# Who makes the low half of the transposed activations: GpSimd or VectorE

## The reference, cut to what matters

```python
mod = (_silu(L0_c) @ L0_wmod).reshape(L0_c.shape[0], 6, 1, -1)
h = _layernorm(x, axis=-1) * (1 + ca) + sa
# _L0_attn_ref(h, ...):
Q = _feature_map(x @ Wq.T + bq); K = _feature_map(x @ Wk.T + bk)   # elu + 1
V = x @ Wv.T + bv
KV = jnp.einsum('bshd,bshe->bhde', K, V)
K_sum = K.sum(axis=1)
Z = 1.0 / (jnp.einsum('bshd,bhd->bsh', Q, K_sum) + 1e-06)
out = jnp.einsum('bshd,bhde,bsh->bshe', Q, KV, Z) @ Wo.T + bo
```

## Time and profile before

| | us |
|---|---|
| median of 3 runs (354.36 to 356.01) | 354.59 |
| the profiled execution | 354.88 |
| its span, first to last instruction | 353.2 |
| TensorE busy | 337.2 (95%) |
| VectorE busy | 283.2 (80%) |
| GpSimd busy | 252.2 (71%) |
| ScalarE busy | 229.7 (65%) |

### The profile page before, as it was taken

One profiled execution on the slowest core, in us unless ns is written; L12 is line 12 of the kernel. 1 busy time (PEld: TensorE's weight loads), 2 busy tenths in 40 slices (PEclk: granted clock), 3 DMA queues, 4 the chain that ended last, 5 costly groups with the idle time before them and its releaser, 6 DMA issues.

```text
span 353.2 us, 7901 instructions
## 1 busy us (share of the span) xinstructions
PE 337.2 (95%) x2487; PEld 316.0 (89%) x2487; DVE 283.2 (80%) x795; ACT 229.7 (65%) x507; POOL 252.2 (71%) x334
## 2 busy tenths in 40 slices
PE   8888999999999997799999999999999999999895
PEld 8666877877888987799999999999999999999895
DVE  4589777657788789998989999898889887886753
ACT  4566778887877755755748558566585585765441
POOL 4348787868977577988879898898899966755210
PEclk9989999999999999999999999999999999999999
DMA  7956510000000033223232232322432333224311
GB/s 262 333 155 182 181 57 0 0 1 2 2 0 1 3 120 122 74 79 119 70 116 90 63 116 90 97 92 62 132 100 65 108 89 105 91 71 141 106 47 59
DMA packets 23998, 31.79 MB, mean 90 GB/s; under 512 B 2310, under 2 KB 14490, under 8 KB 23964
## 3 DMA queue, kind: packets, MB, share of 16 engines
q1 hardware_dynamic: 23524, 31.34, 28.6%
q10 hardware_dynamic: 440, 0.04, 0.1%
HBM read 27.04 MB, written 4.34 MB: 89 GB/s over the span
## 4 chain that ended last, share of the span: by engine, by line
PE 77%; DVE 9%; ACT 6%; POOL 4%; issue 4%; DVEq 0%; POOLq 0%; ACTq 0%
PE bank L867 20%; PE bank L868 20%; PE bank L869 19%; PE bank L875 5%; PE bank L907 4%; PE bank L1048 2%; PE bank L952 2%; PE bank L899 1%; PE bank L1090 1%; ACT tr_f L659 1%; DVE hid_g L1425 1%; POOL rstd L442 1%; ACT e_sb L683 1%; DVE stats L1192 1%; POOL tr_lo L461 1%
## 5 line engine op out<-in xcount | busy, mean ns | idle before, releaser
L805 ACT ACTIVATE bank<-bank,cols_sb 128x256 f32<-128x256 f32 x128 | 51.5, 440 | 49.3 <-PE bank L869 49.1
L867 PE MATMUL bank<-tr_hi,w_hi 128*128 128x256 f32 x256 | 72.7, 284 | 0.0
L869 PE MATMUL bank<-tr_hi,w_lo 128*128 128x256 f32 x256 | 71.6, 280 | 0.0
L868 PE MATMUL bank<-tr_lo,w_hi 128*128 128x256 f32 x256 | 71.6, 280 | 0.0
L867 PE MATMUL bank<-w_hi,hid_pair 128*128 128x256 f32 x252 | 70.8, 281 | 0.0
L868 PE MATMUL bank<-w_lo,hid_pair 128*128 128x256 f32 x252 | 70.6, 280 | 0.0
L869 PE MATMUL bank<-w_hi,hid_pair 128*128 128x256 f32 x252 | 70.6, 280 | 0.0
L552 POOL TENSOR_TENSOR hid_pair<-hid_g,hid_pair 128x512 fp32r<-128x512 f32 x42 | 54.8, 1306 | 4.4 <-ACT hid_pair L812 2.9
L867 PEld LDWEIGHTS bank<-tr_hi,w_hi 128*128 128x128 f32 x256 | 48.5, 189 | 0.3 <-DVE hid_g L1425 0.2
L868 PEld LDWEIGHTS bank<-tr_lo,w_hi 128*128 128x128 f32 x256 | 48.3, 189 | 0.0
L869 PEld LDWEIGHTS bank<-tr_hi,w_lo 128*128 128x128 f32 x256 | 48.2, 188 | 0.0
(11 more groups left out here) (171 smaller groups left out, 910.0 us busy)
## 6 DMA issues: line engine op xcount, KB each, us to landing
g_bc<-g_dram SPq DMA_DIRECT2D x64, 256.0 KB, 3.6
x_sb<-in_x SPq DMA_DIRECT2D x16, 256.0 KB, 3.7
out<-x_sb SPq DMA_DIRECT2D x15, 256.0 KB, 2.3
early<-in_wmod SPq DMA_DIRECT2D x3, 512.0 KB, 6.1
q_sb<-in_w SPq DMA_DIRECT2D x2, 512.0 KB, 6.4
q_sb<-in_w SPq DMA_DIRECT2D x1, 1024.0 KB, 9.4
mod_row<-mod_dram SPq DMA_DIRECT2D x1, 1024.0 KB, 6.3
q_sb<-in_wqkvT SPq DMA_DIRECT2D x2, 256.0 KB, 4.7
```

The source lines that it names most:

```text
L805: last = ac.activation(half, half, ACT.Gelu, bias=b1_sb[:, e:e + 1])
L867: te.matmul(out_ap, l_hi, r_hi, start=start, stop=False, skip_group_check=shared)
L868: te.matmul(out_ap, l_hi, r_lo, start=False, stop=False, skip_group_check=shared)
L869: return te.matmul(out_ap, l_lo, r_hi, start=False, stop=stop, skip_group_check=shared)
```

## The change

`split_lo` goes from GpSimd's program. VectorE's `split_a` makes the low half right behind the high half, and is now called for every unit: for units 9 to 15, whose high half is ScalarE's, it waits for ScalarE (`a_hi_end`) and makes the low half alone. The semaphores that the others wait for stay the same.

```diff
@@ GpSimd
-            def split_lo(u):
-                h = u.h
-                if cast_late(u):
-                    wait(pool, a_hi_end, u.count(1, 1) - (UPB + 1))
-                else:
-                    wait(pool, a_hi, u.count(1, 1))
-                wait(pool, a_qk, u.count(2, -2))
-                gp.tensor_tensor(tr_lo[:, h, :, :], tr_f[:, h, :, :], tr_hi[:, h, :, :].bitcast(F32), ALU.subtract)\
-                  .then_inc(a_lo, 1)
...
-                if u.plus(1):
-                    split_lo(u.plus(1))
@@ VectorE, split_a
                 wait(dve, a_hf, u.count(1, 1))
                 wait(dve, a_qk, u.count(2, -2))
-                ve.tensor_copy(tr_hi[:, h, :, :], tr_f[:, h, :, :]).then_inc(a_hi, 1)
+                if cast_late(u):
+                    wait(dve, a_hi_end, u.count(1, 1) - (UPB + 1))
+                else:
+                    ve.tensor_copy(tr_hi[:, h, :, :], tr_f[:, h, :, :]).then_inc(a_hi, 1)
+                    wait(dve, a_hi, u.count(1, 1))
+                TT(tr_lo[:, h, :, :], tr_f[:, h, :, :], tr_hi[:, h, :, :].bitcast(F32), ALU.subtract).then_inc(a_lo, 1)
@@ VectorE, step_a
-                if u.plus(1) and not cast_late(u.plus(1)):
+                if u.plus(1):
                     split_a(u.plus(1))
```

## The result

The changed kernel takes 357.75 us (median of 6 runs, 357.25 to 358.14) against 354.61 for the kernel before: 1.0082 times as long, 95% interval 1.0064 to 1.0100. It is slower by 3.1 us; 356.4 was forecast, in a range of 352.0 to 359.0.

What follows compares the result with a forecast made beforehand. TensorE was taken to bound the kernel, through its projection-stage gaps. Terms 0 + 0.8 + 1.3 + 0.3 + 0.5 - 1.4 + 0.3 gave +1.8 us: 356.7 for the profiled execution, 356.4 as median, range 352.0 to 359.0.

Steps and rivals of the forecast that it cites:

- What bounds: Projection stage: the change is worth what it does to TensorE's few gaps, 4.8 us of waits for GpSimd's low half.
- The disturbance: VectorE on SBUF: a large GpSimd instruction holds off a subtraction; the 512-element low half ends 0.56 us behind it.
- The small power: GpSimd's 4-element power: by the trace holds no VectorE work; by the page's rule low halves 3 and 11 wait 0.5 us.
- Rival B: The holds don't decide, fewer collisions in sum: 3.3 us gained, 351.3 us, faster; chance 0.14.
- GpSimd is there first by 0.1 to 0.2: Units 5 and 7: the K sum precedes the low half and holds it, +0.65 us each; -0.4 each if VectorE is first.
- The hold of the weight split: Units 6 and 8: delayed sums and biases hold the weight split, which passes 0.15 us on each, +0.3 together.
- rival A: VectorE wins the race in units 5 and 7: 2 x 1.05 us less, 354.3 us; chance 0.22.
- The gain of 0.8 at `place_kv`: Steps 9 and 10: products start 1.3 us earlier, `place_kv` is free, the 0.80 us idle ahead of L1006 goes.
- The gain at `keep_shifts`: Steps 9 and 10: its 1.24 us beside a GpSimd instruction now long done; `kv_of` had waited 0.5 us for it.
- units 10, 13, 14 and 15: within slack: These late units lose 0; VectorE's stand behind ScalarE's high half holds back only what already waited for the exponential.
- rival C: A hold in every unit, low halves of units 11 to 15 too: 2.5 us on top, 358.9 us; chance 0.14.
- rival D: The low half was hidden, another wait of equal length replaces its end at once: 354.6 us; chance 0.08.

Runs made afterwards that it cites:

- experiments 2 and 9: 2: changed kernel, only GpSimd's first K sum waits for unit 2's low half, 356.87 us; 9: changed kernel, VectorE making only low halves 1 to 8, 356.41 us.
- Experiment 8: The changed kernel with one 8-element memset more on GpSimd ahead of the K sum of step 4 alone: 357.77 us.
- experiment 1: The changed kernel with GpSimd's K sum, and all behind it, waiting in each step until VectorE's low half is made: 351.9 us.
- experiment 10: The changed kernel with GpSimd making the low halves of units 1 to 8 as before, VectorE those of units 9 to 15: 355.07 us.

## Why the prediction was right, and where its sizes were off

**What bounds.** TensorE's gaps in the projection stage alone set the price. Right: the rest of the span kept its length within 0.1 us.

**The disturbance.** Right in kind and size. A 512-element low half behind a large GpSimd instruction ends 0.55 behind it (0.56 foreseen). L1276 of the constants (L1284 before) was held at 23.48, as foreseen for step 1. The rows of the kernel after, GpSimd and VectorE in step 1, against the earlier trace rows:

```profile
23.41 1.29 POOL L458 TENSOR_TENSOR hid_g<-hid_g,k_sb 128x512 f32<-128x512 f32 x1
...
23.48 1.36 DVE L1276 TENSOR_SCALAR q_sb<-q_sb 64x256 f32<-64x256 f32 x1
```

It took 0.28 us before and 1.36 now. The small power did not hold a low half: that of unit 3 took its 0.69 us with the power running from 31.75 to 32.93 (kernel after, VectorE, then GpSimd):

```profile
32.40 0.69 DVE L1227 TENSOR_TENSOR tr_lo<-tr_f,tr_hi 128x512 fp32r<-128x512 f32 x1
...
31.75 1.18 POOL L442 TENSOR_TENSOR rstd<-var_eps,minus_half 128x4 f32<-128x4 f32 x1
```

Unit 11's came just behind its power, so that case didn't arise. By the Trainium skill, SBUF — State Buffer, section "Who interferes with whom", whoever issues first has the shared pair for the whole instruction, so that unit 3's low half would have waited to the power's end; the trace decides against that rule for such tiles.

**The sum of the holds.** Rival B argued that 19 us of GpSimd work less make fewer collisions in sum. For VectorE that came true: its busy time without the low halves fell by 1.1 us. The kernel became slower all the same, since the holds moved to places that TensorE waits for.

**Unit by unit.** Units 1 to 6, 9 to 11, 14 and 15 are within 0.25 us of their forecast each. The four that are not:
- *Unit 7* (the step "GpSimd is there first by 0.1 to 0.2"). The margins were 0.02 us in step 4 and -0.05 in step 6, so the steps went apart: +0.68 and -0.40. The step failed since the small last instruction of the deviations (L444), 0.20 us before, was itself held by the cast to 0.47 and 0.40, which the prediction did not count. It ended 0.05 and 0.06 behind the cast. That ties GpSimd's arrival to the end of the cast, where the low half arrives too. The margins are no accident of one execution: experiments 2 and 9 show the same 0.02 and -0.05. Experiment 8 shows that the order of arrival decides, and nothing else that differs between the steps. That unit 5 went as foreseen is luck by the same measure, a margin of 0.02.
- *Unit 8* (foreseen +0.15, measured +0.87). What unit 7 escaped came here: GpSimd's K sum took 1.77, its two sums and biases ran until 61.96, and the cast of unit 8 was held. Timeline of the kernel after, VectorE and GpSimd:

```profile
61.05 1.19 DVE L1225 CAST tr_hi<-tr_f 128x512 fp32r<-128x512 f32 x1 [0.24 <-ACT tr_f L646]
...
60.49 1.47 POOL L464 TENSOR_TENSOR x_sb<-x_sb,mod_row 128x512 f32<-128x512 f32 x1
```

  The hold of the weight split, which the prediction named for this unit, passed nothing on: the cast behind it still waited 0.24 us for ScalarE. Units 7 and 8 together were foreseen at +0.8 and lost 0.47. So rival A (VectorE wins a race) gave less than its price: 1.05 from one race came back by two thirds in the next unit.
- *Unit 12* (foreseen -0.5, measured +0.24). The gain of 0.8 at `place_kv` did not come. The products did start earlier, but the K sum of unit 10, next in GpSimd's queue, moved up as well, to the place where they had been. The rows of the kernel after, against the earlier trace rows:

```profile
83.81 1.28 POOL L458 TENSOR_TENSOR hid_g<-hid_g,k_sb 128x512 f32<-128x512 f32 x1
...
84.18 1.19 DVE L1345 TENSOR_TENSOR early<-early,head_mask 128x256 f32<-128x256 f32 x1
...
85.48 0.51 PEld L993 LDWEIGHTS bank<-wo_sb,early 128*128 128x128 f32 x3 [0.64 <-issue]
```

  The idle time ahead of `make_m` fell from 0.80 to 0.64 only. With GpSimd behind the low half (experiment 1) the gain is there: `place_kv` takes 0.42 us, and unit 12 wins 0.73.

```profile
80.20 0.42 DVE L1347 TENSOR_TENSOR early<-early,head_mask 128x256 f32<-128x256 f32 x1
...
80.83 0.73 PEld L995 LDWEIGHTS bank<-wo_sb,early 128*128 128x128 f32 x4
```

  The low half of unit 12 was held by `make_qz` (1.54 us), as foreseen. The gain at `keep_shifts` did come: L1302 took 0.23 us, and unit 11 won 0.69.
- *Unit 13* (foreseen 0, measured +0.86), and with it the step "units 10, 13, 14 and 15: within slack". Its low half asked at 94.13, and the K sum had come at 94.02:

```profile
94.13 1.70 DVE L1227 TENSOR_TENSOR tr_lo<-tr_f,tr_hi 128x512 fp32r<-128x512 f32 x1 [0.49 <-ACT tr_hi L654]
...
94.02 1.27 POOL L458 TENSOR_TENSOR hid_g<-hid_g,k_sb 128x512 f32<-128x512 f32 x1
...
96.62 0.19 PEld L854 LDWEIGHTS bank<-hid_pair,tr_hi 128*128 128x128 f32 x1 [0.99 <-DVE tr_lo L1227]
```

  Here rival C was right for one unit: a large instruction that has started just before the low half asks. Units 14 and 15 were within slack. Unit 10 was not quite: it lost 0.18, and as much in experiment 1, without holds. In the changed kernel the exponential was ready at 75.34, but the low half ended at 75.65 and the map started at 75.57. So the low half did keep the map back by some 0.2 us, which the prediction had ruled out.

**The sum.** +1.8 was foreseen, and the unit starts give +3.1; unit 12 (0.74), unit 13 (0.86) and the pair 7 and 8 (-0.33) make 1.27 of the 1.31 missing. The mechanism, its main places and the sign were right, the size was a little over half. The median came out 1.35 us above the forecast for the same reasons. Rival B (holds don't decide) is refuted by experiment 1, rival D by the table. B's price of 3.3 us for a change without holds was nearly right as a size: experiment 1 has 2.7.

**What stays open.** Experiment 1 has GpSimd wait in every step. Whether a wait in fewer steps, those alone in which a hold reaches TensorE, would do better than 351.9 was not tried. The 0.10 us at unit 1 is explained in part: TensorE's weight load starts 0.12 us behind the end of the feature map, which now ends last, where it had started 0.05 behind the low half; why is not shown.

## What to carry to other kernels

When work leaves an engine, ask what that engine will do in its place: its queue moves up, and here the instructions that moved up cost the kernel more than the move gained (5.8 us against 2.7). The sum of the holds doesn't show it, as that hardly changed; their places do. Between GpSimd and VectorE on SBUF, keep large GpSimd instructions out of the moment in which VectorE has work that TensorE waits for; one semaphore wait that orders them was worth 5.85 us, though it adds idle time. Margins of some 0.1 us in such an order could not be forecast from durations here, so price both outcomes, and look for what a dodged hold hits next.

## What the runs showed of the hardware

- Which of the two engines is held follows the order of arrival down to 0.02 to 0.05 us: 44.12 against 44.14 gave GpSimd 1.27 and VectorE 1.80; 56.14 against 56.09 and, in experiment 8, 44.02 against 43.99 gave VectorE 0.69 and GpSimd 1.77 and 1.80. In the traces of all the runs together a low half on VectorE and a GpSimd instruction on 128 x 512 start within 0.15 us of each other 27 times; each time the one recorded second is the one that is held.
- GpSimd gives way between two instructions in a row: with the low half of unit 5 waiting, the K sum ended at 45.39, the low half at 45.94, and the next GpSimd instruction, recorded from 45.35, took 1.72 instead of 1.29.
- A 4-element GpSimd instruction can be held by VectorE's cast (0.47 instead of 0.20 us) and by its low half (0.75, experiment 10), though it holds neither: the cast took 0.43 and the low half 0.69.
- A VectorE instruction that was held ended as long behind GpSimd's each time: 0.54 to 0.55 us for the 512-element low half (units 5, 9, 12 and 13), 0.28 to 0.29 for the 256 elements of `place_kv`.
